# A transformer chain on one core: linear product moved beside the probabilities' product, query and norm transposes joined in one run, mean row's copies put behind the last pairs

## What is computed

```python
for i in range(4):                                   # DEPTH
    x = x + self_attention(layer_norm(x, ...), ...)  # 8 heads of 32
    h = layer_norm(x, ...)
    x = x + (gelu(h @ W1[i] + b1[i]) @ W2[i] + b2[i])
...
def self_attention(x, Wq, Wk, Wv, Wo, bo):
    lo = local_attn(q[:, :4], k[:, :4], v[:, :4])            # softmax, windows of 128
    go = causal_linear_attn(q[:, 4:], k[:, 4:], v[:, 4:])    # softmax(q) times running context
    return concat(lo, go) @ Wo + bo
...
x = _layernorm(x0 + that)
x = _layernorm(x + cross_attention(x, context))
x = _layernorm(x + gelu(x @ W1c) @ W2c)              # W1c, W2c: weighted sums of 32 low-rank products each
```

## Time and profile before

| | |
|---|---|
| median of 3 runs | 972.21 us (971.94 to 974.06) |
| profiled execution | 972.99 us |
| its span | 971.3 us |
| PE busy | 953.5 us, 98% of the span |
| DVE, ACT, POOL busy | 667.8, 613.0, 480.2 us |
| mean granted TensorE clock | 0.998 |
| time of the chain that ended last on PE | 90%; DVE 6%, ACT 2% |

### The profile page before, as it was taken

The page is one execution under the profiler, slowest core; times in us unless marked ns, Lnnn a source line. Parts: engine busy times, 40 slices in busy tenths (PEclk is TensorE's granted clock), DMA queues, the critical chain, the costliest instruction groups (busy, mean ns, idle before and its releaser), DMA issues.

```text
span 971.3 us, 21328 instructions
## 1 busy us (share of the span) xinstructions
PE 953.5 (98%) x8421; PEld 819.2 (84%) x8421; DVE 667.8 (69%) x1466; ACT 613.0 (63%) x1392; POOL 480.2 (49%) x381
## 2 busy tenths in 40 slices
PE   7989999999999999999999999999999999999998
PEld 4668888888888988888888888888898869998987
DVE  7696767667776868677677768686452766676545
ACT  4777777676786777776867867777735345444220
POOL 3446465367816564774646277733427224006443
PEclk9999999999999999999999999999999999999999
DMA  6111000002010000021000002001048696720001
GB/s 208 53 38 45 3 16 2 18 1 88 1 45 17 2 1 18 1 88 45 18 2 1 19 1 88 1 2 49 2 96 200 145 185 133 177 60 1 22 23 44
DMA packets 71582, 47.56 MB, mean 49 GB/s; under 512 B 44511, under 2 KB 68159, under 8 KB 71487
## 3 DMA queue, kind: packets, MB, share of 16 engines
q1 hardware_dynamic: 71487, 46.27, 18.5%
HBM read 44.16 MB, written 2.10 MB: 48 GB/s over the span
## 4 chain that ended last, share of the span: by engine, by line
PE 90%; DVE 6%; ACT 2%; issue 1%; DMA 0%; POOL 0%; SPq 0%; POOLq 0%; ACTq 0%; DVEq 0%
PE F L1441 21%; PE F L1595 17%; PE A L1441 16%; PE A L1768 5%; PE A L1775 5%; PE A L1540 4%; PE A L1933 4%; PE A L1557 2%; PE F L1455 2%; PE A L1498 2%; PE A L1455 2%; PE F L1434 1%; PE A L1434 1%; PE A L1531 1%; PE A L1514 1%; DVE smax L694 1%
## 5 line engine op out<-in xcount | busy, mean ns | idle before, releaser
L1441 PE MATMUL F<-xt,w 128*128 128x512 f32 x864 | 217.8, 400 | 0.2 <-ACT scratch L1195 0.2
L462 POOL TENSOR_TENSOR ht<-scratch,ht 128x512 fp32r<-128x512 f32 x128 | 176.2, 1398 | 38.4 <-ACT ht L1198 36.8
L1441 PEld LDWEIGHTS F<-xt,w 128*128 128x128 f32 x864 | 157.7, 188 | 38.3 <-issue 3.0
L1595 PE MATMUL F<-w,ht 128*128 128x256 f32 x1536 | 189.3, 282 | 0.0
L1595 PEld LDWEIGHTS F<-w,ht 128*128 128x128 f32 x1536 | 182.9, 188 | 5.3 <-issue 4.6
L450 POOL TENSOR_TENSOR rstd<-var,minus_half 128x4 f32<-128x4 f32 x32 | 37.6, 1175 | 179.8 <-DVE var L598 179.4
L1195 ACT ACTIVATE scratch<-F,b_now 128x512 f32<-128x512 f32 x128 | 87.6, 684 | 36.6 <-POOL ht L462 19.6
L1441 PE MATMUL A<-wa,xt 128*128 128x512 f32 x372 | 89.8, 397 | 0.0
L457 POOL TENSOR_TENSOR x<-x,vec_f 128x1024 f32<-128x1024 f32 x16 | 38.0, 2372 | 93.0 <-DVE scratch L618 93.0
L1198 ACT ACTIVATE ht<-scratch 128x512 fp32r<-128x512 f32 x128 | 81.0, 633 | 4.1
L1441 PEld LDWEIGHTS A<-wa,xt 128*128 128x128 f32 x372 | 69.0, 188 | 15.9 <-issue 0.2
(11 more groups left out here) (259 smaller groups left out, 2041.7 us busy)
## 6 DMA issues: line engine op xcount, KB each, us to landing
raw_f<-in_L_attn_W_dram SPq DMA_DIRECT2D x8, 1024.0 KB, 5.9
scratch<-in_L_ffn_fc_B_dram SPq DMA_DIRECT2D x32, 256.0 KB, 4.6
scratch<-in_L_ffn_fc_A_dram SPq DMA_DIRECT2D x32, 256.0 KB, 3.9
raw_f<-in_L_ffn_fc_A_dram SPq DMA_DIRECT2D x32, 64.0 KB, 3.4
scratch<-in_x_dram SPq DMA_DIRECT2D x1, 2048.0 KB, 10.5
raw_f<-in_L_ffn_fc_B_dram SPq DMA_DIRECT2D x32, 64.0 KB, 3.2
x<-in_x_dram SPq DMA_DIRECT2D x3, 512.0 KB, 7.4
out_dram<-x SPq DMA_DIRECT2D x3, 512.0 KB, 2.9
```

What stands on the lines that cost most here:

```text
L462: pool.tensor_tensor(ht[:, 1, m, :], hf[:, m % 2, :], ht[:, 0, m, :].bitcast(F32), ALU.subtract).then_inc(h_lo, 1)
L1441: last = pe.matmul(out, lhs(a, c), rhs(b, c), start=clear and k == 0, stop=k == len(total) - 1, skip_group_check=not clear)
L1595: last = pe.matmul(F[:, t % 2, 0:D], ht[:, a, c, P * t:P * t + P], w2[:, b, c, :], start=k == 0, stop=k == len(passes) - 1)
```

## The change

It does four things. In regular steps (n from 2 to 15) PE's query transposes move from before the second scores to behind y(3), and there join both halves of the MLP's input transposes and the probabilities' transposes; the wait for `ctxn_done` now stands before them. The linear product moves from between the halves to the place before the probabilities' product and writes bank A 0, so that `pe_pv` needs no wait for its copy. The copies follow: ACT's query copy goes behind the first probabilities' copy, ACT's and DVE's copies of the linear product behind those of the local heads. At the composed weights, ACT's copy of the mean row goes behind `pair_hi` of the last two pairs and DVE's part behind that item's variance. Steps 0 and 1 keep their order.

```diff
@@ -679,12 +679,15 @@
                               kcum[:, :, :].rearrange("p b (j o) -> p b j o", o=1).broadcast_to([P, 2, 3, E]),
                               ALU.mult).then_inc(ctxn_done, 1)
 
+        def lin_bank(n):
+            return A[:, 1 if n < 2 else 0, :]
+
         def later_buckets(ap):
             return ap.rearrange("p (b t) -> p b t", b=2)[:, :, BUCKET:T]
 
         def dve_lin_lo(dve, n):
             dve.wait_ge(lin_hi, n + 1)
-            lo(dve, later_buckets(at[:, 1, 1, :]), later_buckets(A[:, 1, :]),
+            lo(dve, later_buckets(at[:, 1, 1, :]), later_buckets(lin_bank(n)),
                later_buckets(at[:, 0, 1, :])).then_inc(lin_lo, 1)
 
         def dve_max(dve, n, b):
@@ -924,6 +927,8 @@
                 norm_var(q, p)
                 if f == 1 and count == 2:
                     f_xt_lo_part(0)
+                if f == 0 and count == 2:
+                    mean_rows_lo()
                 if count > 2:
                     pair_lo(f, first + 2, 4)
                 norm_scale(q, p, range(2), False)
@@ -969,7 +974,6 @@
                 if mlp:
                     dve_xt_lo(dve, 1, n - 1)
                 if attn:
-                    dve_lin_lo(dve, n)
                     dve_pt(dve, n, 0)
                 if nxt:
                     dve.wait_ge(res2, 4 * (n + 1) + 4)
@@ -986,6 +990,7 @@
                     dve_xt_lo(dve, 0, n + 1)
                 if attn:
                     dve_al_lo(dve, n)
+                    dve_lin_lo(dve, n)
                 else:
                     pair_lo(0, 1, 1)
                 if attn:
@@ -1051,8 +1056,6 @@
                     first_big_lo(3, 3)
 
             for q in range(ITEMS):
-                if q == ITEMS - 1:
-                    mean_rows_lo()
                 pairs_lo(0, 4 * q + 2, 4 if q < ITEMS - 1 else 2, q, q)
             for u in range(2 * ITEMS):
                 dve.wait_ge(t_bout, u + 1)
@@ -1157,7 +1160,7 @@
 
         def act_lin_hi(act, n):
             act.wait_ge(lin_psum, n + 1)
-            act.activation(later_buckets(at[:, 0, 1, :]), later_buckets(A[:, 1, :]), ACT.Copy).then_inc(lin_hi, 1)
+            act.activation(later_buckets(at[:, 0, 1, :]), later_buckets(lin_bank(n)), ACT.Copy).then_inc(lin_hi, 1)
 
         def act_exp(act, n, b):
             act.wait_ge(smax_done, 2 * n + b + 1)
@@ -1258,7 +1261,6 @@
                     act_features(act, n)
                     act_exp(act, n, 0)
                     act_seed(act, n, 1)
-                    act_qnt(act, n)
                     act_exp(act, n, 1)
                 else:
                     for k in range(4):
@@ -1284,9 +1286,9 @@
                                        ACT.Copy).then_inc(cross_hi, 1)
                 act_xt_hi(act, 1, n - 1)
                 if attn:
-                    act_lin_hi(act, n)
                     act_pspread(act, n)
                     act_pt(act, n, 0)
+                    act_qnt(act, n)
                 if p % ITEMS == 1:
                     act_b1(act, l + p // ITEMS)
                 gelu(0, 1)
@@ -1299,6 +1301,7 @@
                 gelu(2, 3, 4)
                 if attn:
                     act_al_hi(act, n)
+                    act_lin_hi(act, n)
                 gelu(5)
                 if nxt:
                     act_xt_hi(act, 0, n + 1)
@@ -1390,11 +1393,11 @@
             with act.Fori(0, ITEMS - 1) as i:
                 for j in range(4):
                     pair_hi(0, 4 * i + 2 + j, 2 + j)
+            for kk in (PAIRS - 2, PAIRS - 1):
+                pair_hi(0, kk, kk % 4)
             act.wait_ge(mean_zero, 2)
             act.wait_ge(mean_psum, 1)
             act.activation(mean_row[0][0:B, :], F[0:B, 0, 0:D], ACT.Copy).then_inc(mean_row_hi, 1)
-            for kk in (PAIRS - 2, PAIRS - 1):
-                pair_hi(0, kk, kk % 4)
             act.wait_ge(pair_done, PAIRS)
             act.wait_ge(t_sum, ITEMS)
             for k in range(4):
@@ -1501,7 +1504,6 @@
             last.then_inc(s_psum, 1)
 
         def pe_qnt(pe, n):
-            pe.wait_ge(kf_done, n + 1)
             pe.wait_ge(qn_done, n + 1)
             for t in range(TILES):
                 last = pe.transpose(A[:, 0, P * t:P * t + P], qexp[:, t, :], ident[:, :])
@@ -1514,6 +1516,7 @@
                     last = pe.matmul(A[E * h:E * h + E, b, j * HB:(j + 1) * HB], kexp[0:rows, t, E * h:E * h + E],
                                      v8[0:rows, t, NH + h, :], start=start, stop=stop, skip_group_check=True)
                 return last
+            pe.wait_ge(kf_done, n + 1)
             for b in range(2):
                 part(b, 2, 2 * b, P, True, False)
                 part(b, 1, 2 * b, P, False, False)
@@ -1528,7 +1531,7 @@
                     cols = slice(b * T + u * BUCKET, b * T + (u + 1) * BUCKET)
                     for h in range(NH):
                         r = slice(E * h, E * h + E)
-                        last = pe.matmul(A[r, 1, cols], ctxn[r, b, u - 1, 0:E], qnt[r, cols], start=True, stop=True)
+                        last = pe.matmul(lin_bank(n)[r, cols], ctxn[r, b, u - 1, 0:E], qnt[r, cols], start=True, stop=True)
             last.then_inc(lin_psum, 1)
 
         def pe_pt(pe, n, b):
@@ -1550,7 +1553,8 @@
         def pe_pv(pe, n):
             pe.wait_ge(pt_out_act, 2 * n + 2)
             pe.wait_ge(pt_out_dve, 4 * n + 4)
-            pe.wait_ge(lin_lo, n + 1)
+            if n < 2:
+                pe.wait_ge(lin_lo, n + 1)
             for b in range(2):
                 for t in range(2):
                     for h in range(NH):
@@ -1820,11 +1824,11 @@
                     y(0)
                     y(1)
                     y(2)
-                    pe_qnt(pe, n)
                     pe_s(pe, n, 1)
-                    pe.wait_ge(qnt_out, n + 1)
                     pe_ctx(pe, n)
                     y(3)
+                    pe.wait_ge(ctxn_done, n + 1)
+                    pe_qnt(pe, n)
                 else:
                     context((0, 1))
                     y(0)
@@ -1835,10 +1839,7 @@
                     y(3)
                 pe.wait_ge(res2, RES2_0 + 4 * (n - 1) - 1)
                 pe_xt(pe, 1, n - 1, (0,))
-                if attn:
-                    pe.wait_ge(ctxn_done, n + 1)
-                    pe_lin(pe, n)
-                else:
+                if not attn:
                     pe.wait_ge(cross_hi, 2)
                     turn(0, 0, 0)
                     turn(0, 1, 1)
@@ -1848,10 +1849,13 @@
                     pe_pt(pe, n, 0)
                 h(0, 1)
                 if attn:
+                    pe.wait_ge(qnt_out, n + 1)
                     pe_pnorm(pe, n)
                     pe_pt(pe, n, 1)
                 h(2, 3)
                 if attn:
+                    pe.wait_ge(pnorm_out, n + 1)
+                    pe_lin(pe, n)
                     pe_pv(pe, n)
                 h(4, 5)
                 if nxt:
```

## The result

| | before | changed |
|---|---|---|
| median | 971.79 us (6 runs) | 976.14 us (6 runs) |
| ratio, 95% interval | | 1.0052 (1.004 to 1.0064) |
| profiled execution, its span | 972.99, 971.3 us | 976.11, 974.4 us |

The changed kernel is slower by 4.35 us, 0.45%. The forecast was 2.1 us slower, half of that. The time lies in the range.

The account below looks back on a forecast made before the run. PE, 98% busy, was taken to bound the kernel, with the scores-to-h(0) chain next in line. Regular steps +6.0 us and the mean row -3.9 gave +2.1, a median of 974.3 us, range 970.5 to 977.5.

Parts of the forecast that it names:

- The chain behind the scores is next in line: Regular steps, second scores' end through maxima and exponentials to h(0): needs 6.69 us, against 6.19 of PE's own work.
- The query transposes start the chain 0.42 sooner; late steps gain nothing: Before the second scores: scores end 0.42 us earlier in eight steps; where DVE reaches the maxima late, nothing starts earlier.
- The linear product keeps its 0.80 and pays it all: Before the probabilities' product: the same 24 products take 0.80 us, all on the path, with no extra switch cost taken.
- The moved copies cost nothing: ACT's and DVE's moved copies in regular steps: taken as 0, bounds 0 and 0.21 us in each of 13 steps.
- Step 5 gives 0.3: Step 5: PE's unexplained 1.10 us stall becomes hidden under the chain, against 0.80 added, about 0.3 us less.
- The mean row gives 3.9: Composed weights, mean product to cross products: 10.86 us becomes some 7.0, 3.9 less, some 1.7 of it slow clock.
- The sum: Whole kernel: steps +6.0 us and mean row -3.9 give +2.1, a median of 974.3 us.
- (a): Regular steps: PE's list decides alone, each of 14 gains 0.21 us; with the mean row 965.4 us; chance 0.16.
- (b): Before gelu(5): ACT's linear copy delays the next queries, 0.21 us in 13 steps above forecast, 977.0 us; chance 0.14.
- (d): Mean row: gives less because the clock falls behind the narrow product anyway, 976.0 us; counted within the forecast's 0.60.
- (c): Regular steps: clock falls at the new 0.5 us wait behind long transposes, some 1.7 us each, 998 us; chance 0.04.

Follow-up runs that it names:

- the experiment with the shorter chain: Maxima made two heads at a time, so exponentials start sooner: in the changed kernel 968.22 us, ratio 0.9965; in the kernel before 971.81 us, ratio 0.9999.

## Why the prediction was right, and where its size was off

- **The chain behind the scores is next in line.** Right, in its place and its size. h(0) at 6.69 in steps like step 10 was forecast and measured, and the experiment with the shorter chain gave 8 us back where PE was waiting and nothing where it was not.
- **The query transposes start the chain 0.42 sooner; late steps gain nothing.** Right: 0.44 less idle in front of DVE in step 10, and in step 11 an h(0) that did not move. The kernel without this move was 3.5 us slower in the medians and 3.1 in the profile, forecast 3.4.
- **The linear product keeps its 0.80 and pays it all.** Right: 0.80 in the new place, no more for the switch between narrow tiles of two shapes.
- **The moved copies cost nothing.** This term of the sum was mis-sized. I took 0 and kept 0.21 in each of 13 steps as a bound. It was 0.05 in each of 13 (the first queries' product takes 1.45 in step 10, where it took 1.40), and 0.38 in step 15, which I had not looked at by itself: h(4) to h(7) takes 6.09 there instead of 5.71. Together 1.0: the steps cost 7.1 in the profile, not 6.0.
- **Step 5 gives 0.3.** It gave nothing: from its scores' end to the next step's it is 45.78 (235.91 to 281.69), where it was 45.76 (235.09 to 280.85). The stall of 1.10 is gone, but DVE is late there as in steps 9 and 13: h(0) stands 7.67 behind the scores in all three, and these two cost 0.94 and 0.95, not 0.80. In some of the eight early steps the cost was less than forecast (0.22 to 0.23 in steps 4, 8 and 12), so this does not show in the total.
- **The mean row gives 3.9.** Right for the profiled execution (3.8), wrong for the median, which is what was to be forecast: alone it gave 2.05 (2.5 by the ratio), and taking it out of the changed kernel cost 2.15. The step that failed is that I counted the stretch at clock 0.50 as belonging to every execution. I had written down that 1.7 of the 3.9 was the slow clock (measured, 1.5) and didn't ask whether it comes each time; the stretch with the idle but without the fall, 9.33 us, shows that it doesn't.
- **The sum.** +7.1 and -2.1 would be +5.0; measured are +4.35. The forecast's +2.1 was short by 1.0 for the copies and 1.8 for the mean row. That gives 4.9; the rest to 4.35 is within the interval, some 1.2 us to either side.
- **The rivals.** (a), PE alone deciding, is out for this kernel. With short maxima h(0) comes 6.26 behind the scores in step 10, near the 6.19 of PE's own work, but the order then gains 0.25 us over the old one in the profile and not 2.9. (b) had the right mechanism at a quarter of its price: ACT copies the next input 5.10 behind h(4) (478.55 to 483.65), where it was 4.88, so 0.22 later and under the 0.3 that (b) asked for. (d) named 976.0, and 976.14 was measured, but its mechanism did not come: with the mean row's copy moved, the clock behind the narrow product stays at 1.00 in the changed kernel. That the medians lie so near (b)'s and (d)'s numbers is luck. (c) did not come: with runs of 24 transposes and a wait inside them in all 14 steps, the clock stayed up in the changed kernel.

```profile
51.00:800.00 749.00, 738.43 (x6797) 630.30 (x6796) 516.71 (x1106) 517.30 (x1188) 396.69 (x288) 1.00 0.15 37
```

What the Trainium skill (TensorE: Matmul & The Clock Gate, Part 4: PE-mode transpose) says of transposes and the clock had no effect here that could be seen.

## What to carry to other kernels

An engine that is busy for 98% of the span can still be one short step from a wait: before work is taken out of a stretch, measure the chain that runs beside it from the same start, because only the difference is gained, while the work put elsewhere is paid in full. Move work out of such a stretch together with what shortens the chain: with the mean row's part in both, the changed kernel lost 4 us without the short chain and was 3.5 under before with it, of which the mean row's part makes some 2. And a cost read in one profiled execution, above all a stretch of lower clock, has to be weighed by how often it comes before it is counted for the median. One more profile is not enough: here two of three with the idle have the fall.

## What was not expected of the hardware

The same idle of 1.55 us at the same place was followed by a granted clock of 0.50 for 3.4 us in two profiled executions and by none in a third. The fall costs 1.4 to 1.5 us there (10.77 and 10.86 against 9.33).

A wait can be nearly invisible in the list of waits: in step 10 the row shows 0.18 idle, while the starts are 0.40 further apart than the work needs.
